# A Mamba and mixture-of-experts layer on one core: Softplus' round-off term moved from VectorE to ScalarE and GpSimd, the carries of three scans kept by ScalarE

## The reference, cut to what matters

```python
dt = jax.nn.softplus(jnp.einsum('blr,dr->bld', dt, W_dt) + b_dt)   # 512 channels
A = -jnp.exp(A_log)                                               # 16 states
def step(h, inputs):
    dA = jnp.exp(dt_t[:, :, None] * A[None])
    dBu = (dt_t * u_t)[:, :, None] * B_t[:, None, :]
    h = dA * h + dBu
    y = jnp.einsum('bdn,bn->bd', h, C_t)
```

## Time and profile before, and how to read it

| what | us |
|---|---|
| time, median of 3 runs | 2477.61 (2473.47 to 2480.32) |
| time of the profiled execution | 2465.4 |
| its span, first to last instruction | 2463.6 |
| VectorE busy | 2106.2 (85%) |
| PE busy | 1941.2 (79%) |
| GpSimd busy | 1818.6 (74%) |
| ScalarE busy | 1693.5 (69%) |

### The profile page before, as it was taken

One profiled execution on the slowest core, in us unless ns is written; L12 is line 12 of the kernel. 1 busy time (PEld: TensorE's weight loads), 2 busy tenths in 40 slices (PEclk: granted clock), 3 DMA queues, 4 the chain that ended last, 5 costly groups with the idle time before them and its releaser, 6 DMA issues.

```text
span 2463.6 us, 35833 instructions
## 1 busy us (share of the span) xinstructions
PE 1941.2 (79%) x8902; PEld 1091.0 (44%) x8902; DVE 2106.2 (85%) x2976; ACT 1693.5 (69%) x3289; POOL 1818.6 (74%) x1211
## 2 busy tenths in 40 slices
PE   4566767677988699877988689886989689676996
PEld 1212223133655265534655256443655256454664
DVE  0299999999999999999899999999899998999533
ACT  3677777677887668866787678867787678654343
POOL 0478776987778987888778887888778886967232
PEclk9888778787999899988999899998999899888998
DMA  7545444356889588868978598867978588898554
GB/s 200 121 104 111 113 103 112 97 135 170 229 221 226 152 230 230 230 153 202 249 199 235 137 235 232 223 158 192 249 212 227 149 219 222 237 230 260 178 158 131
DMA packets 269867, 460.01 MB, mean 187 GB/s; under 512 B 37472, under 2 KB 120032, under 8 KB 269536
## 3 DMA queue, kind: packets, MB, share of 16 engines
q1 hardware_dynamic: 257376, 424.09, 66.3%
q0 software_dynamic: 12288, 33.64, 4.6%
HBM read 355.24 MB, written 102.34 MB: 186 GB/s over the span
## 4 chain that ended last, share of the span: by engine, by line
PE 37%; DVE 23%; issue 15%; ACT 15%; POOL 5%; DMA 3%; SPq 1%; ACTq 0%; POOLq 0%; DVEq 0%
DVE dA L1053 12%; PE ring L573 6%; PE ring L582 6%; PE p_g L712 5%; ACT dA L930 4%; PE ring L599 4%; PE yps L680 3%; DVE arena L1053 3%; PE ring L638 2%; DVE arena L1064 2%; PE p_a L692 2%; POOL arena L1263 2%; DMA tok<-sorted_y,pos 1%; PE p_a L757 1%; PE yps L676 1%
## 5 line engine op out<-in xcount | busy, mean ns | idle before, releaser
L1263 POOL TENSOR_TENSOR arena<-arena,b_bc 128x2048 f32<-128x2048 f32 x256 | 979.6, 3826 | 79.3 <-PE yps L680 59.8
L930 ACT ACTIVATE dA<-arena,a_s 128x512 f32<-128x512 f32 x1024 | 675.2, 683 | 159.8 <-DVE arena L1064 135.9
L1053 DVE TENSOR_TENSOR_SCAN dA<-dA,carry,arena 128x512 f32<-128x512 f32 x384 | 478.0, 1275 | 10.5 <-ACT dA L930 10.0
L1053 DVE TENSOR_TENSOR_SCAN dA<-dA,arena 128x512 f32<-128x512 f32 x384 | 454.8, 1215 | 25.4 <-ACT dA L930 25.4
L680 PE MATMUL yps<-arena,const_s 128*32 128x512 f32 x2048 | 311.2, 682 | 156.5 <-POOL arena L1271 92.5
L1271 POOL TENSOR_TENSOR arena<-arena,c_bc 128x511 f32<-128x511 f32 (+1 forms) x256 | 289.2, 1130 | 182.2 <-DVE arena L1053 179.2
L712 PE MATMUL p_g<-xT,w_e 128*128 128x128 f32 x2448 | 330.0, 293 | 45.1 <-DVE hT L1170 45.0
L712 PEld LDWEIGHTS p_g<-xT,w_e 128*128 128x128 f32 x2448 | 320.6, 208 | 75.8 <-issue 72.6
L573 PE MATMUL ring<-arena 128*128 128x512 f32 x512 | 278.0, 669 | 60.8 <-ACT sz L851 35.6
L1064 DVE TENSOR_TENSOR arena<-dA,c_bc 128x1024 f32<-128x1024 f32 x256 | 312.3, 1220 | 4.4
L582 PE MATMUL ring<-arena 128*128 128x512 f32 x512 | 238.6, 609 | 9.8 <-ACT arena L842 5.8
(11 more groups left out here) (136 smaller groups left out, 3116.2 us busy)
## 6 DMA issues: line engine op xcount, KB each, us to landing
arena<-dt_d SPq DMA_DIRECT2D x512, 256.0 KB, 6.6
w_e<-in_w_moe SPq DMA_DIRECT2D x153, 512.0 KB
w_e<-in_w_moe SPq DMA_DIRECT2D x153, 256.0 KB, 5.3
dt_d<-arena SPq DMA_DIRECT2D x128, 256.0 KB, 3.6
xt<-sorted_x SPq DMA_DIRECT2D x191, 128.5 KB
sorted_y<-yt SPq DMA_DIRECT2D x191, 128.0 KB
b_bc<-bc_d SPq DMA_DIRECT2D x256, 64.0 KB, 4.2
c_bc<-bc_d SPq DMA_DIRECT2D x256, 64.0 KB, 3.5
```

What stands on the lines that cost most here:

```text
L930: act.activation(dA[:, j, :], rep_dt[:, c % 2, j, :], ACT.Exp, scale=a_s[:, n, j:j + 1]).then_inc(s_exp, 1)
L1053: return dve.tensor_tensor_scan(out_ap, dA[:, j, :], hs[:, u % 3, j, :], init, ALU.mult, ALU.add)
L1263: pool.tensor_tensor(hs[:, u % 3], rep_dtu[:, c % 2], b_bc[:, g, :].unsqueeze(1).to_broadcast([P, J, T]), ALU.mult).then_inc(s_dbu, 1)
```

## The change

ScalarE makes 1 + e as before and then 1 - (1 + e) in a second instruction; GpSimd adds e to that, which gives the negative of the old term, and `less_lost` adds it where it subtracted. VectorE's `round_off` is gone. GpSimd's stands ahead of `less_lost`, `scatter` and `gather` in its slot, in the same slots as VectorE's had. The copies into `carry` of scans 0, 1 and 2 are gone from VectorE; ScalarE makes them, `keep01` at the start of its slot and `keep2` ahead of decay 2, in even chunks. The decays of the next unit wait for these copies, and the scans of odd chunks wait for the semaphores of the copies.

```diff
@@ scalar: exp_abs
-                act.activation(t_s[:], dtub[:, c % 2, :], ACT.Identity, bias=1.0).then_inc(s_s, 1)
+                act.activation(t_s[:], dtub[:, c % 2, :], ACT.Identity, bias=1.0).then_inc(s_one, 1)
+                act.wait_ge(s_one, v + 1)
+                act.activation(t_s[:], t_s[:], ACT.Identity, bias=1.0, scale=-1.0).then_inc(s_s, 1)
@@ scalar: decay
+                if u > 0 and (u - 1) // UN % 2 == 0 and j != 3:
+                    act.wait_ge(s_carry01 if j < 2 else s_carry2, UN * ((u - 1) // UN // 2) + (u - 1) % UN + 1)
                 act.activation(dA[:, j, :], rep_dt[:, c % 2, j, :], ACT.Exp, scale=a_s[:, n, j:j + 1]).then_inc(s_exp, 1)
+
+            def keep01(u):
+                act.wait_ge(s_m01, u + 1)
+                act.activation(carry[:, u % UN, 0:2], dA[:, 0:2, T - 1], ACT.Copy).then_inc(s_carry01, 1)
+
+            def keep2(u):
+                act.wait_ge(s_m2, u + 1)
+                act.activation(carry[:, u % UN, 2:3], dA[:, 2, T - 1:T], ACT.Copy).then_inc(s_carry2, 1)
@@ scalar: the loop over slots
+                if 0 <= s < UN * NQ and q % 2 == 0:
+                    keep01(s)
                 if 0 <= s + 1 < UN * NQ:
                     decay(s + 1, 1)
...
+                if 0 <= s < UN * NQ and q % 2 == 0:
+                    keep2(s)
                 if 0 <= s + 1 < UN * NQ:
                     decay(s + 1, 2)
@@ vector
-                if j == 3 and not first:
-                    dve.wait_ge(s_carry3, UN * (q // 2) + n + 1)
+                if not first:
+                    dve.wait_ge((s_carry01, s_carry01, s_carry2, s_carry3)[j], UN * (q // 2) + n + 1)
...
-                if q % 2 == 0:
-                    dve.tensor_copy(carry[:, n, 0:2], dA[:, 0:2, T - 1]).then_inc(s_carry, 1)
...
-                if q % 2 == 0:
-                    dve.tensor_copy(carry[:, n, 2:3], dA[:, 2, T - 1:T]).then_inc(s_carry, 1)
...
-            def round_off(q, c):
-                dve.wait_ge(s_s, CC * q + c + 1)
-                dve.scalar_tensor_tensor(t_s[:], t_s[:], 1.0, dtub[:, c % 2, :], ALU.subtract, ALU.subtract).then_inc(s_t, 1)
@@ gpsimd
+            def round_off(q, c):
+                pool.wait_ge(s_s, CC * q + c + 1)
+                pool.tensor_tensor(t_s[:], t_s[:], dtub[:, c % 2, :], ALU.add).then_inc(s_t, 1)
...
-                pool.tensor_tensor(dtub[:, c % 2, :], dtub[:, c % 2, :], t_s[:], ALU.subtract).then_inc(s_sub, 1)
+                pool.tensor_tensor(dtub[:, c % 2, :], dtub[:, c % 2, :], t_s[:], ALU.add).then_inc(s_sub, 1)
...
                 if n == 3 and 0 <= q - 1 < NQ:
                     deviation(1, q - 1)
+                for c, at in enumerate((-9, -5, 0, 4)):
+                    if (s - at) % UN == 0 and 0 <= (s - at) // UN < NQ:
+                        round_off((s - at) // UN, c)
```

More of the change, by code:

```diff
@@ L302, in mamba_moe @@
         s_s = sem("s_s")
+        s_one = sem("s_one")
         s_l = sem("s_l")
@@ L314, in mamba_moe @@
         s_scan = sem("s_scan")
-        s_carry = sem("s_carry")
+        s_carry01 = sem("s_carry01")
+        s_carry2 = sem("s_carry2")
         s_m01 = sem("s_m01")
@@ L1190, in _ @@
                     unit_third(s)
-                for c, at in enumerate((-9, -5, 0, 4)):
-                    if (s - at) % UN == 0 and 0 <= (s - at) // UN < NQ:
-                        round_off((s - at) // UN, c)
                 for g, k in tiles_in(s - 2):
```

## The result

The changed kernel took 2505.93 us (median of 4 runs, 2497.66 to 2513.14), the kernel before 2476.9 beside it: a ratio of 1.0116, 95% interval [1.0081, 1.0151]. Measured again, in 5 runs beside 23 of the kernel before, it was 1.0156 [1.0136, 1.0176]: 2509.28 against 2468.81 us. So the change costs 29 to 40 us by the medians; the forecast was 2513 us, 36 us slower. The time is near the forecast. Several of the terms that made it up are not, as is told further down.

A forecast was written before the change was run, and what follows sets the result against it. VectorE and ScalarE take turns in bounding the loop, ScalarE leading about 11 of 16 even-chunk slots. Five chunk pairs 37.5 us, start +1.3, first four chunks about 0, final two -3: +36 us on 2477.6, 2513 us; range 2460 to 2545.

The forecast's parts named there:

- VectorE's relief decides: Rival, chance 0.2: ScalarE's copies fall into its idle time, about half of VectorE's 73 us comes through, 2445 us.
- VectorE's relief, 73 us: On VectorE: 37 us of round-off steps, 16 of stalls inside them and 20 for 256 carry copies.
- The forecast's signs: What would show it, among others: VectorE's busy time down by about 95 us, its idle time up by more.
- last pair: Last two chunks: even one +4.6 us less about 2.2 of a stall, odd one about 5.5 back; -3 us.
- ScalarE's additions, 98 us: On ScalarE: 64 Identity instructions at 0.66 us, 42 us, and 256 carry copies at 0.22 us, 56 us.
- 2.0 us per even chunk: Three of an even chunk's four Softplus steps fall where ScalarE leads, each passing on the second Identity's 0.66 us.
- An even chunk, +4.6 us: ScalarE's additions pass on: copies 4.8 us in about 11 slots, Identities 2.0, less 0.2, 1.0 and 1.0.
- The wait before 1224.07: VectorE's 2.46 us wait in an even chunk should grow by about 0.6 us.
- An odd chunk, +2.9 us: No copies: +0.3 us from ScalarE's and VectorE's shifts, +2.6 from GpSimd's late scatter and gathers in slot 7.
- passes on whole: Odd chunk, slot 7: the second gather's 2.6 us delay reaches scan 3 in full; ends 0 and up to 5.
- GpSimd's new wait ahead of the gathers: Rival, chance 0.15: in five odd chunks the gathers land 5 us later than by issue alone, 2538 us.
- Both cancel: Rival, chance 0.1: half of the chains are absorbed, no change, 2478 us.

The follow-up runs named there:

- relief_only: Kernel before without VectorE's round-off steps and its carry copies of scans 0 to 2, given to no engine; odd-chunk scans start from 0: 2443.09 us, 0.9842.
- ident_added: Kernel before plus a second ScalarE Identity that copies t_s onto itself, for which VectorE's round-off waits: 2498.77 us, 1.0123.
- keep_twice: Changed kernel with each of ScalarE's carry copies made twice, the second behind a wait for the first: 2535.48 us, 1.0267 against the kernel before.
- ro_only: Kernel before with only the round-off term moved to ScalarE and GpSimd as in the change, carries staying on VectorE: 2481.42 us, 1.0014.
- relief_ro: Kernel before without VectorE's 64 round-off steps, nothing added on another engine: 2448.01 us, 0.9914.
- ro_last: Changed kernel with GpSimd's round-off addition moved to the end of its slot: 2499.19 us, 1.0125 against the kernel before.
- pool_all: Kernel before with the round-off term wholly on GpSimd as two instructions, ScalarE and carries as before: 2478.26 us, 0.9994.

## Why the prediction was right, and where it was not

**The reading of what bounds the kernel** held. Freed time on VectorE turned into waits for ScalarE (118.9 to 157.4 us), and the even chunks, where ScalarE leads, got longer. The rival "VectorE's relief decides" fell by its sign. Its estimate that half of the 73 us comes through (36, where its sum takes off 33) looks like what `relief_only` measured, but that kernel had 23 us more taken off; alone, the two reliefs gave 21 and 3 us, a third of 73.

**VectorE's relief, 73 us.** The busy time fell by 77 us (69 in the second profile). The forecast's signs said 95, against its own sum: a copy and the step behind it overlap by 0.08 us, and the page counts that time once, so 73 was to be expected. Worth alone: 21 us for the round-off term against 53 counted, 3 us for the copies against 20. The stalls of the earlier trace rows vanished with L1083, as forecast; the last pair's odd chunk came out 6.0 and 7.5 us shorter, forecast 5.5. The Trainium skill ("SBUF — State Buffer", "SBUF: two separate sides") calls the shared access an exclusive lock that a VectorE instruction with two SBUF inputs takes too. The rows of `ident_added` agree: a 0.67 us step took 4.01 us, until 0.55 us past the end of GpSimd's, which had begun first.

**ScalarE's additions, 98 us.** Its busy time rose by 79. A copy costs 0.28 us to the next start in the median, not 0.22, so 70 us and not 56. `keep_twice` shows over half of such additions on the path. The second Identity lasts 0.63 us as taken, and costs what was said where ScalarE leads: 0.65 us in slot 0 and 0.66 in slot 4 of `ro_only`, and 0.61 in slot 7 (8.64 against 8.03 us in `relief_ro`) where both have the low clock in slot 6. So the 2.0 us per even chunk are 1.3 to 1.9. That `ro_only` is only 0.6 us longer in all has another reason, the 1.3 us of the clock in slot 14 that the kernel before pays and it does not.

**An even chunk, +4.6 us,** held, and by its mechanism: with slots 5, 6 and 14 at the full clock it is 4.4 us. The shares are less exact. The forecast's terms give 3.1 us for the carries (4.8 - 0.2 - 1.0 and three slots' 0.16) and 1.4 for the round-off term; alone they made 2.3 and 0.8, and 1.3 more together. What the forecast did not have is TensorE's clock. It makes the measured difference 3.1 to 3.3 us in one profile, where the kernel before paid 1.3 us in slot 14 and the changed one did not, and 6.0 to 6.7 in the other, where slot 5 cost 1.66 us more and slot 7 in two chunks 0.6. That the forecast lies between the two is so for this reason. The wait before 1224.07 of 2.46 us should grow by 0.6: it is 3.02 us (the row at 1246.96), nearly that, and 4.68 at the low clock.

**An odd chunk, +2.9 us**, was wrong. Chunks 7, 9 and 11 grew by 0.5, -0.1 and 0.3 us (1.0, 0.6 and 0.3 in the second profile). The step that failed is the one by which the gather's delay "passes on whole". GpSimd's and TensorE's timelines of slot 7 after:

```profile
1405.11 1.09 POOL L1282 TENSOR_TENSOR t_s<-t_s,arena 128x512 f32<-128x512 f32 x1 [1.13 <-ACT t_s L873]
...
1408.96 0.96 POOL L1319 DMA_INDIRECT tok<-sorted_y,pos  x1 [0.30 <-issue]
```

```profile
1414.40 2.05 PE L640 MATMUL ring<-tok,const_s 128*128 128x256 f32 x4 [1.26 <-DMA tok<-sorted_y,pos]
```

From the chunk's first multiplication the second gather is issued 2.2 us later (68.7 against 66.5 us), as said. But its data were there 5.4 us after the issue and not 8.9, and TensorE's sum starts 1.4 us earlier in the chunk than before (74.2 against 75.5). The landing did not follow the issue; that was the lower bound of the text, 0, and it should have been the value taken. By what it was set instead no run here isolates. With it falls the rival "GpSimd's new wait ahead of the gathers", which had them land later. But GpSimd's step was not free, as the forecast had it elsewhere: it delays `weigh` of slot 11, and slot 13 grows from 8.2 us to 9.0 or more. The Identity adds 0.6 in slot 4. VectorE's relief pays for most of both, with 0.6 us each in slots 0 and 7, and slot 9 came out 0.2 to 0.7 shorter (all from the first profile).

**Sum.** The five pairs (chunks 4 to 13) were put at 37.5 us. They gave 22.7 in the first profile and 34.1 in the second. The last pair was put at -3 and gave -0.5 and -1.8. The rest of the two spans' difference lies where the forecast had put 1.3 us: chunks 0 to 3 gave 8.4 and 3.3 us, start and tail 8.7 and 8.8. So the mechanism of the even chunk was right, and that the total came out so near was in part luck: the odd ones had 14.5 us for five and gave 5.2 and 4.0, and these stretches made up for it. "Both cancel" is true of the round-off half (1.0014) and not of the carries.

**Open.** The whole costs 29 to 40 us, its halves 12. In the steady even chunks the difference is 1.3 us in slots 7 and 8 and the low clock of slot 5, as shown; for slot 8 the reason was not settled. In chunks 0 to 3 the first profile has 12 us more than the halves together (8.4 against -4.1 and 0.0), but the second profile of the same kernel only 7, so single profiles can't settle these. Nor is it known which of the two profiles the timed runs resemble.

## What to carry to other kernels

Where two engines lead by turns, work moved from the busier one costs what it adds where the other leads, and the relief turns into waits: lay the timelines side by side, and count contacts of some 0.03 us as waits. A short instruction between two that depend on it costs its time to the next start, here 0.28 us for 0.16 busy. And before pricing a delay of a DMA's issue, ask whether its landing follows its issue at all.

An added or removed step is not measured by itself as long as some other instruction can stall on its timing: look at the mean duration of the groups that should not have changed. And before two profiles are subtracted, TensorE's granted clock has to be compared stretch by stretch: here it made the even chunks of one kernel differ by 3 us between two executions, as much as the whole change in one of them.

## What the runs showed that was not expected

- **Stalls move.** The same 64 round-off steps took 58.2, 67.4, 68.6 and 87.3 us of VectorE in four kernels that do not alter them, since their start moved against GpSimd's. Two small edits' times (+31 and -3 us) were in part this.
- **TensorE's clock is part of the path.** After the same wait of 2 us the same group of 6 matmuls took 1.56 us in one execution and 2.44 in another of the same kernel. Each of these two kept its pattern over even chunks 6 to 12; in `ro_last` and `keep_twice` it changed from one to the next.
- **Start and tail vary.** From the span's start to the first multiplication it took 108.9 to 119.8 us, from the last one to the end 168.9 to 177.6 us, over 14 profiled executions with nearly the same work there. A span alone can't decide about 10 us in this kernel.
- **GpSimd, 74% busy, has little slack in one place.** A step in the middle of its slot makes slot 13 of every odd chunk from 5 to 13 longer (one in `ro_only`, chunk 7, excepted), and 118 us more work there (`pool_all`) used up 21 us of relief.
